# Second LayerNorm of a ViT block: the four normalising operations move from VectorE to ScalarE

## The reference, cut to what matters

```python
def _layernorm(x, axis=-1, eps=1e-05):
    m = jnp.mean(x, axis=axis, keepdims=True)
    v = jnp.var(x, axis=axis, keepdims=True)
    return (x - m) / jnp.sqrt(v + eps)

h = tokens(x)                                   # 64 images, 65 tokens each, 128 features
h = h + attention(_layernorm(h))
z_in = _layernorm(h)                            # the ffn normalises again, with scale and bias:
flat = (z_in - mu) * rsqrt(var + eps) * ln_scale + ln_bias
h = h + shared_ffn(flat) + routed_experts(flat) # gates, top-2 of 4 experts in one of 2 groups
```

## Time and profile before

| what | value |
|---|---|
| median of 3 runs | 526.9 us (526.65 to 529.51) |
| the profiled execution's own time | 527.09 us |
| its span, first to last instruction | 525.1 us |
| mean granted clock of TensorE | 0.949 of full |
| PE busy | 478.2 us, 91% of the span |
| DVE busy | 319.8 us, 61% |
| ACT busy | 184.6 us, 35% |
| POOL busy | 174.1 us, 33% |

### The profile page before, as it was taken

The page is one execution under the profiler, slowest core; times in us unless marked ns, Lnnn a source line. Parts: engine busy times, 40 slices in busy tenths (PEclk is TensorE's granted clock), DMA queues, the critical chain, the costliest instruction groups (busy, mean ns, idle before and its releaser), DMA issues.

```text
span 525.1 us, 7237 instructions
## 1 busy us (share of the span) xinstructions
PE 478.2 (91%) x2322; PEld 322.8 (61%) x2322; DVE 319.8 (61%) x869; ACT 184.6 (35%) x342; POOL 174.1 (33%) x213
## 2 busy tenths in 40 slices
PE   5999996999999999999999999999968797898974
PEld 2355555855775577656765577557756575687562
DVE  0043346365877577675767586758667758764672
ACT  0026214541174225621463127322842273223120
POOL 6012301220371118311641155204721552137054
PEclk9989996799999999999999999999989896989788
DMA  8996570046004520253015400000000010000001
GB/s 336 353 413 216 189 218 30 0 134 223 13 1 141 171 79 2 82 179 127 1 41 180 166 0 20 0 0 0 20 2 0 1 21 1 0 2 2 20 0 22
DMA packets 14413, 44.71 MB, mean 85 GB/s; under 512 B 1721, under 2 KB 7090, under 8 KB 14386
## 3 DMA queue, kind: packets, MB, share of 16 engines
q1 hardware_dynamic: 12882, 42.39, 24.3%
q10 hardware_dynamic: 1504, 1.99, 1.1%
HBM read 42.24 MB, written 2.13 MB: 85 GB/s over the span
## 4 chain that ended last, share of the span: by engine, by line
PE 68%; DVE 15%; issue 7%; POOL 4%; DMA 3%; SPq 3%; ACT 1%; DVEq 0%; POOLq 0%
PE acc L421 22%; PE O L511 5%; PE B L407 4%; PE scores L485 4%; DMA x_main<-in_x_main 3%; DVE z_nat L1085 2%; SPq L385 2%; PE B L464 2%; PE C L588 2%; PE B L450 2%; PE C L562 2%; PE B L445 2%; PE C L563 2%; PE scores L623 1%; PE C L564 1%
## 5 line engine op out<-in xcount | busy, mean ns | idle before, releaser
L421 PE MATMUL acc<-x_main,w_patch 128*128 128x512 f32 x288 | 140.2, 616 | 6.6 <-DMA w_patch<-in_w_patch 6.0
L421 PEld LDWEIGHTS acc<-x_main,w_patch 128*128 128x128 f32 x288 | 51.4, 194 | 51.6 <-issue 41.7
L1572 POOL TENSOR_TENSOR prod<-prod 128x512 f32<-128x512 f32 (+1 forms) x33 | 42.7, 1294 | 18.8 <-DVE prod L1298 18.8
L511 PEld LDWEIGHTS O<-v_bd,probs_t 128*128 128x128 f32 x256 | 32.8, 195 | 23.0 <-ACT probs_t L844 11.6
L844 ACT ACTIVATE probs<-shift 128x512 f32<-128x512 f32 x32 | 20.2, 630 | 74.0 <-DVE shift L1137 74.0
L1565 POOL TENSOR_TENSOR hidden_lo<-silu,hidden_hi 128x512 fp32r<-128x512 f32 (+1 forms) x18 | 20.9, 1163 | 76.0 <-ACT hidden_hi L844 75.9
L511 PE MATMUL O<-v_bd,probs_t 128*128 128x64 f32 (+1 forms) x256 | 34.9, 280 | 4.9 <-ACT probs_t L844 4.9
L1133 DVE TENSOR_REDUCE row_max<-scores 128x8 f32<-128x520 f32 x32 | 22.3, 698 | 22.1 <-PE scores L485 21.9
L844 ACT ACTIVATE probs_t<-B 128x512 f32<-128x512 f32 x32 | 19.0, 594 | 43.8 <-PE B L407 43.2
L1534 POOL TENSOR_TENSOR p_cls<-exp_cls,row_rec 128x16 f32<-128x16 f32 x16 | 3.5, 222 | 91.1 <-DVE row_rec L1153 91.1
L1298 DVE TENSOR_TENSOR prod<-scores,comb 128x512 f32<-128x512 f32 (+1 forms) x33 | 22.5, 683 | 17.0 <-POOL routed L1579 13.2
(11 more groups left out here) (251 smaller groups left out, 1009.4 us busy)
## 6 DMA issues: line engine op xcount, KB each, us to landing
x_main<-in_x_main SPq DMA_DIRECT2D x48, 768.0 KB, 4.3
out_tokens<-y_out SPq DMA_DIRECT2D x16, 128.0 KB, 2.5
w_patch<-in_w_patch ACTq DMA_DIRECT2D x6, 192.0 KB, 9.9
prod<-in_w_eout SPq DMA_DIRECT2D x2, 512.0 KB
x_tail<-in_x_tail SPq DMA_DIRECT2D x8, 96.0 KB, 3.5
silu<-in_w_in SPq DMA_DIRECT2D x2, 256.0 KB
hidden<-in_rows ACTq DMA_DIRECT2D x1, 256.0 KB, 15.8
w_attn<-in_w_attn ACTq DMA_DIRECT2D x1, 256.0 KB, 17.2
```

What stands on the lines that cost most here:

```text
L421: last = mm(acc[:, :], w_patch[:, j, :], x_main[:, j, :], start=(j == 0), stop=False)
L511: last = mm(O[:, c:c + 64].rearrange("p (b c) -> p b c", b=2), probs_t[p % 2][:, hp * 128:(hp + 1) * 128], pair, start=True, stop=True)
L1572: q.tensor_tensor(p[r, 0, :], p[r, 0, :], p[r, 1, :], ALU.add).then_inc(tree1_done.sem, 1)
```

## The change

ACT computes `z = rstd * h + shift` with its Identity function, a scale and a bias per row. DVE prepares the bias for all tiles in one small instruction, `shift2 = -mean * rstd`. `z_done` is then signalled by ACT. ACT's four instructions stand behind `normed_t(g+1)`, at the end of the body, ahead of `z_out(g)` where there is one; in the class part behind `shared_out(7)`.

```diff
+        shift2 = sb("shift2", [128, TILES])
...
+            def z_scale(g, src, tiles, rows):
+
+                need(act, shift2_done, g)
+                need(act, zt_full, g - 1)
+                for t in range(tiles):
+                    go(z_nat[0:rows, t * 128:(t + 1) * 128], src[0:rows, t * 128:(t + 1) * 128], ACT.Identity,
+                       scale=rstd2[0:rows, t:t + 1], bias=shift2[0:rows, t:t + 1]).then_inc(z_done.sem, 1)
...
                 if nxt:
                     normed_t(g + 1)
+                z_scale(g, h2[par], TILES, 128)
                 if last:
                     z_out(g, TOK)
...
             shared_out(L, TOK)
+            z_scale(GROUPS, h2[0], 1, IMAGES)
             z_out(GROUPS, IMAGES)
...
-            def norm2_scale(g, src, tiles, rows):
+            def norm2_scale(g, tiles, rows):
                 need(dve, rstd2_done, g)
-                normalise(z_nat, src, mv2, rstd2, z_done, tiles, rows)
+                v.scalar_tensor_tensor(shift2[0:rows, 0:tiles], mv2[0:rows, 0, 0:tiles], -1.0, rstd2[0:rows, 0:tiles],
+                                       ALU.mult, ALU.mult).then_inc(shift2_done.sem, 1)
```

More of the change, by code:

```diff
@@ L266, in vit_tower @@
         bn2_done, mv2_step = ev("bn2_done", TILES), ev("mv2_step", 6)
-        var2_done, rstd2_done = ev("var2_done"), ev("rstd2_done")
+        var2_done, rstd2_done, shift2_done = ev("var2_done"), ev("rstd2_done"), ev("shift2_done")
         z_done, zt_full, zt_done = ev("z_done", TILES), ev("zt_full"), ev("zt_done", 2)
@@ L1463, in body @@
                     weigh(g - 1, 1, 128)
-                norm2_scale(g, h2[par], TILES, 128)
+                norm2_scale(g, TILES, 128)
                 if last:
@@ L1484, in _ @@
             weights(L, TILES, 128)
-            norm2_scale(GROUPS, h2[0], 1, IMAGES)
+            norm2_scale(GROUPS, 1, IMAGES)
             shared_add(L, h2[1], TILES, 128)
```

## The result

The changed kernel takes 533.0 us (median of 6 runs, 530.05 to 534.13) against 526.8 of the kernel before beside it (523.72 to 529.51): ratio 1.0119 [1.0081, 1.0157]. It is slower by 6 to 7 us; I had said 2, and at most 4.6 (531.5).

The account below looks back on a forecast made before the run. PE, busy 91% of the span, was taken as the bound. Groups 1 to 6 -1.4, group 0 +2.3 and class tokens +1.1 gave +2.0 us on 527.1, 529.1, stated as 529.0; 8-in-10 range 526.0 to 531.5.

Parts of the forecast that it names:

- Part 1: Groups 1 to 6: `shift2` held by POOL's sum, transposes hardly earlier, a later PE wait gone; 1.4 us gained in all.
- The term was 0.23 us a group: Groups 1 to 6: transposes start 0.05 us earlier and `expert(g-1, 6)` saves its 0.18 us wait for the weighing.
- DVE's earlier weighings: Groups 1 to 6: later weighings come over 1 us earlier, but PE waits for none of them; counted as nothing.
- Part 2: Group 0 into group 1: ACTIVATEs ahead of ACT's table load delay `k_t` and `z_t`, so PE loses 2.3 us.
- the waits at 1.5 and 2.3 us: Group 1: PE waits 1.5 us for `k_t` at `k_sums`; gates run 2.3 us later in all, the 1.5 included.
- the clock's return hangs on `ffn_in`: Group 0 into group 1: full clock returns 3.07 us after the first 128x512 `ffn_in` matmul, now at 102.0.
- Part 3: Class tokens: the ACTIVATE stands behind `shared_out(7)`, so PE's transpose starts 1.13 us later; 1.1 us lost.
- so the whole 1.1 us is lost: Class tokens: nothing queued behind PE's delayed transpose has slack, so the delay passes fully into the time, 1.1 us.
- no extra cost: Group 0 into group 1: the clock returns equally long after the `ffn_in` matmul, adding nothing to the 2.3 us.
- rival 2: Slower by the clock: group 1's hole adds a low stretch, 530.7 us; the tail's another, 532.4; chance 0.33.
- low stretches recur wherever PE has holes: Argument for extra low-clock stretches after new PE holes in group 1 (+1.7 us) and in the tail.
- one sign in my own rows: Before `ffn_in(0)`: clock at 0.50 though PE was busy 3.36 of 3.41 us; taken as pointing to `ffn_in` alone.

Follow-up runs that it names:

- lock_off: The changed kernel, with POOL waiting for `shift2` before it starts the experts' sum: 529.55 us, ratio 1.0024 to the kernel before.
- best: both_lock plus three discarded matmuls in the tail's hole and five between group 0 and 1: 516.75 us, ratio 0.9817 to the kernel before.
- both_lock: The changed kernel with group 0 and class tokens normalised by DVE again, and POOL's sum waiting for `shift2`: 520.40 us, ratio 0.987 to the kernel before.

## Why the prediction was wrong

**Part 1, groups 1 to 6: right in mechanism, low in size.** `shift2` was held 1.25 us, as `e_group` had been, the four ACTIVATEs took 1.65 us for my 1.59, and the date of the transposes stayed. The Trainium skill's "SBUF — State Buffer", section "Who interferes with whom", speaks of such an exclusion between a DVE instruction with two SBUF inputs and a GpSimd instruction that reads SBUF: the trace agrees at 1.25 us for a 128x4 operation, and lock_off turns it off by order alone (0.16). The term was 0.23 us a group; the period fell by 0.31 in the profile (55.14 to 54.83 us in the mean), and the middle as a whole gained 2.8 to 3.3 us where I had 1.4. The term that I had at nothing is the spacing of the expert matmuls: two in a row start 0.240 to 0.241 us apart in the mean, from group 1's statistics to group 5's, in all eleven profiles with ACT there, and 0.244 in the three with DVE; 43 times a group, that makes 0.17 us. Why they come closer isn't shown (I had given DVE's earlier weighings nothing), nor is what groups 5 to 7 add.

**Part 2, group 0: the waits were right, the clock wasn't.** I had the waits at 1.5 and 2.3 us; they are 1.38 and 2.30, and the distance to group 1 grew by 2.15. `k_t` stands 0.11 us behind the table load's small instruction, as I had said. At equal clock the part costs 2.6 to 3.3 for my 2.3. Over many runs its price is 3.9 to 4.3, and the profiles agree: from group 0 to group 1 the six with group 0 on ACT ahead of the table load take 55.6 to 56.6 us, mean 56.3, and the six with it on DVE 50.6 to 54.7, mean 52.2. The former have 17.1 to 20.5 us of low clock there, the latter 10.2 (three), 17.1 (two) and 20.5 (one). So more low clock is usual there, not certain. My reading that the clock's return hangs on `ffn_in` doesn't hold either. In the three DVE profiles with 10.2 us it was back 4.8 to 5.3 us ahead of the first `ffn_in` matmul, and stayed. In five of the six with ACT it was back over 7 us ahead of it, and fell again after 3.4 us, for 6.8 or 10.2 us more.

**Part 3, class tokens: the hole was right, its price wrong.** The hole is 1.23 us for my 1.13. The step that failed is "so the whole 1.1 us is lost", together with "I take it that it comes back the same time after that matmul [...]: no extra cost" in part 2: in the sum the clock stood at zero. In its place the runs show a low stretch of 10.2 to 13.7 us in the tail instead of 3.4, that is 5.7 to 6.1 us for the part, and 3.9 to 4.3 for group 0 in place of 2.3. This is rival 2, which had 0.33 and named both places, with 532.4 for both. It sized the tail at one stretch more; there were three more.

The reason that rival 2 gave, "low stretches recur wherever PE has holes", was too simple as well: in the trace of before the clock fell at 464.95 and at 485.42 behind stretches in which PE was busy for 3.42 of 3.42 us, with 59 and 55 short matmuls.

I had one sign in my own rows. In the earlier trace rows PE was busy in 3.36 of 3.41 us and the clock stayed at 0.50; I read that as a reason why it might hang on something else, and made "no extra cost" the likeliest. With a price of several us on one side and about one on the other, the sum should have carried part of it.

**What stays open.** Why the clock returns after one stretch in one tail and after three or four in the other isn't settled. A hole of 1.2 us, some ten us ahead of the one of 2.9, goes with the difference in every profile (the first two rows of the table against the third and fourth), and filling the later hole takes it away. But the later hole also lies differently in them: in the 3.41 us before the clock fell PE was busy for 0.47 to 0.79 us in the four profiles with the long low stretch, and for 1.54 to 1.90 in the six with the short one. Whether the early hole itself counts, or only that it moves the later one, no run here separates. What the chip looks at in deciding wasn't measured.

## What to carry to other kernels

A move to another engine is worth what it does to that engine's list: here the same ACTIVATEs gave 533.2 or 525.6 us in the mean, over 7 us apart, depending on whether they stood ahead of a table load and behind one unrelated copy, or the other way round. Where a DVE operation with two SBUF inputs starts beside a POOL instruction, look who goes first before moving anything: one wait in POOL's list gave 1.1% with the work left where it was. And price a new hole on PE at more than its length where stretches near it stand at 0.50: here holes of 1.2 and 2.3 us cost about 6 and 4.

## What the runs showed of the hardware

- The time of this kernel moves with the time its TensorE spends at 1.2 GHz by 0.36 us per us. Most of the spread of the kernel before, 523.7 to 530.8 us without its four longest executions, goes with it.
- The clock stayed at 1.2 GHz for 13.7 us in which PE was busy for 3.41, 3.42, 2.75 and 3.41 us of its four stretches.
- Matmuls whose result is thrown away took the low stretches out of two places (eight of them, in best), and PE was busy for less time with more instructions than in the kernel before. How much of best's 3.6 us over both_lock is theirs rests on one profile and six runs of each, and the intervals of the two ratios overlap; three of them in the tail of the kernel before alone gave 0.9984, not told from zero.
- A 128x4 operation of DVE with two SBUF inputs, 0.16 us alone, took 1.25 us when it started 0.07 us behind a POOL `tensor_tensor` of 1.30 us; with POOL made to wait for it, 0.16 again, in a POOL wait of 0.35.
- An ACTIVATE of 128x128 out of SBUF with a scale and a bias per row took 0.48 to 0.50 us, four in a row 1.65.
